# The feed-forward's shift by one token: DMA between rows of X in place of transposes there and back

## The chip, the cores and the metric

The kernel runs on one core of one Trainium2 chip. The metric is the device time of one execution in microseconds. A NeuronCore has five engines, each with an instruction stream of its own: TensorE (PE: matrix multiplications and transposes into PSUM; PEld is its weight load), VectorE (DVE), ScalarE (ACT), GpSimd (POOL) and SyncE (SP, which here issues all DMAs). Their streams meet through semaphores. DMA transfers run on 16 engines of their own. X is 4 batches of 1024 tokens with 128 channels, in float32; a tile is 128 tokens of one batch, and tokens lie on the 128 partitions of the on-chip memory (SBUF).

## The reference

After an attention block, a residual and a layernorm, six layers run on x of shape (4, 1024, 128):

```python
def shift_tokens(t):
    a, s = jnp.split(t, 2, -1)
    s = jnp.pad(s, ((0, 0), (1, 0), (0, 0)))[:, :-1]
    return jnp.concatenate([a, s], -1)

for i in range(DEPTH):   # 6
    x = attn_layer(shift_tokens(x), Wqkv[i], q_scale[i], k_scale[i], Wo[i]) + x   # 16 heads of 64, window 32
    x = ffn_layer(shift_tokens(x), ln_g[i], ln_b[i], W1[i], b1[i], W2[i], b2[i]) + x

def ffn_layer(x, g, bln, W1, b1, W2, b2):
    xn = (x - mu) / jnp.sqrt(var + 1e-05) * g + bln
    a, gate = jnp.split(xn @ W1 + b1, 2, -1)          # 2 x 341 columns
    return a * jax.nn.gelu(gate, approximate=False) @ W2 + b2
```

The shift before the feed-forward is what the change is about: channels 0 to 63 of a token stay, channels 64 to 127 come from the token before (zeros for the first token of a batch).

## The kernel before

`layers` (L872) holds the six layers. X stays in SBUF as [128 tokens, batch, tile of the sequence, channel]. Work goes in slots: slot s = 4 u + d, where u counts steps (8 blocks of 128 tokens in each of 6 layers, 48 steps) and d = 0 to 3. Each engine has its own loop over the slots (LAST_SLOT = 204) with the order of its tasks written out by hand, and the tile is processed as a pipeline over slots: in slot s tile s is projected to q, k and v, tile s-1 is rotated, normalised and transposed, tile s-2 is scored, tile s-3 attended, and tile s-4 goes through the output projection, which VectorE adds to X (`output`, L1602; semaphore `xd`). There are two PSUM tensors for pairs (PA, PB), one for the scores and the feed-forward (PC) and one for transposes and the output (PD).

The feed-forward of a step needs all four batches of it. The attention output of step u-1 is complete early in slot d = 3 of step u, and there the feed-forward starts, in these places of the loops:

- TensorE, between the lone transpose `input_T(s + 1)` (L1202) and `project_v` (L1210): `ff_shift` transposes X of four batches to PC (L1299), so that channels lie on partitions. After `project_v`: `ff_tokens` transposes back (L1308). In the slot before (d = 2) nothing stands between these.
- ScalarE: `ff_carry` (L1472) puts the last token of the step before, kept in FS, in front; `ff_shift` (L1478, L1479) copies PC to FS, channels 64 to 127 one column on.
- VectorE: `ff_tokens` (L1608) copies PC to fx; `ff_stats` (L1613 to L1621) takes mean and variance; then `input_T(s + 1)` (L1548) makes the residual of the next tile's transposed input, in two halves, for which TensorE waits at `project_qk` of the next slot; then `ff_down(u - 2)` (L1644), `ff_scale` (L1626) and, in the next slot, `sums` and `output`.
- GpSimd, at d = 0 of the next step: `frs_power` (L1108) takes the root of the variance, ahead of `norms` (L1125 to L1131), `normalise` (L1138), `divide` (L1114), `normalise`. TensorE's second group of q/k transposes (L1236) in that slot waits for the second `normalise`.
- TensorE goes on with the feed-forward one and two slots later (`ff_norm`, L1317, at d = 1).

SyncE issues DMAs in order. In a slot: `values_in(s - 1)`, four loads of VW from DRAM (L1052; each 32 rows of four pieces of 2 KB), which wait until the attention of tile s-3 has read the other buffer (semaphore `pv`); then `values_out(s)`, the store of V (L1040; 128 rows). At d = 0 a share of the next layer's weights (L1033) is loaded, and once a layer at d = 0 the feed-forward's weights and biases (L1027): W1, W2 in two pieces (the second 85 rows), b1 in three (128, 128 and 85 rows of two elements of 4 bytes), b2 (one row) and the two of the layernorm (128 rows of 4 bytes). In the first attention stage `max_rows` (L490) moves 8 rows of 256 bytes from SBUF to SBUF in each DMA.

Of the kernel before, what the change touches and what calls it, by code (L numbers as in the profile page):

```python
# [10 lines left out]
ACT = mybir.ActivationFunctionType  # L11
AX = mybir.AxisListType

P = 128
B, S, D = 4, 1024, 128
NT = S // P
# [855 lines left out]
def layers(nc, ins, w):  # L872
# [6 lines left out]
    m = Memory(nc)  # L879
    X, ident, ident_b, gate_b = w["X"], w["ident"], w["ident_b"], w["gate_b"]  # L880
# [34 lines left out]
    VW = m.sb("VW", [P, 2, NW, 512])  # L915
    ET = m.sb("ET", [P, PAIRS, P])
    OT = m.sb("OT", [P, PAIRS, P])
    FS = m.sb("FS", [P, B, P + 1])
    fx = m.sb("fx", [P, B, D])
    fst = m.sb("fst", [P, B, 6])  # L920
    fmv = m.sb("fmv", [P, B, 2])
# [49 lines left out]
    oe = m.count("l_oe")  # L971
    wo = m.count("l_wo")
    xd = m.count("l_x1")
    f1 = m.count("l_f1")
    f1e = m.count("l_f1e", 2)
    fc = m.count("l_fc")
    f2 = m.count("l_f2")
    f2e = m.count("l_f2e")
    fsd = m.count("l_fst", 3)
    fr = m.count("l_frs")  # L980
# [19 lines left out]
    def is_tile(n):  # L1000
        return 0 <= n < TILES

    def is_step(u):
        return 0 <= u < STEPS
# [8 lines left out]
    def on_sp(sp):  # L1013

        def load_ff(l):
            for dst, src in (
                (W1[:, :], ins["W1"][l]),
                (W2[:, 0:2, :], ins["W2"][l, 0:2 * P].rearrange("(a p) n -> p a n", p=P)),
                (W2[0:FF - 2 * P, 2, :], ins["W2"][l, 2 * P:FF]),
                *((b1[0:c, :, i], ins["b1"][l].rearrange("(i f) -> f i", i=2)[lo:lo + c])  # L1020
                  for i, (lo, c) in enumerate(CH)),
                (W2[LASTW:LASTW + 1, NCH - 1, :], ins["b2"][l].unsqueeze(0)),
                (ln[:, 0:1], ins["ln_g"][l].unsqueeze(1)),
                (ln[:, 1:2], ins["ln_b"][l].unsqueeze(1)),
            ):
                with nc.allow_non_contiguous_dma("small columns"):
                    sp.dma_start(dst, src).then_inc(s_wf.sem, 16)  # L1027

        def load_share(u):
            t, l = u % NT, u // NT  # L1030
            if u > 0:
                sp.wait_ge(wsp.sem, wsp.at(u - 1))
            sp.dma_start(Wraw[:, :], ins["Wqkv"][l + 1][:, t * share:(t + 1) * share]).then_inc(s_wr.sem, 16)  # L1033

        def values_out(n):
            u, b, t, l = tile(n)
            sp.wait_ge(ve.sem, ve.at(n))
            if n >= TILES // NL:
                sp.wait_ge(vw[n % 2].sem, vw[n % 2].at((n - B) // 2))
            sp.dma_start(v_dram[b, WIN + t * P:WIN + (t + 1) * P], Vs[:, :, :]).then_inc(vd.sem, 16)  # L1040

        def values_in(n):
            u, b, t, l = tile(n)
            p = n % 2
            sp.wait_ge(vd.sem, vd.at(n))
            if n >= 2:
                sp.wait_ge(pv.sem, pv.at(n - 2))
            for c in range(2):
                rows = v_dram[b, t * P + c * WIN:(t + 1) * P + c * WIN].rearrange("(v r) a n -> r v a n", r=WIN)
                for a in range(2):  # L1050
                    lo = a * KW + c * WIN
                    sp.dma_start(VW[lo:lo + WIN, p, :, :], rows[:, :, a, :]).then_inc(vw[p].sem, 16)  # L1052

        sp.wait_ge(s_one.sem, READY)
        for b in range(B):
            sp.dma_start(v_dram[b, 0:WIN], kH[0:WIN, :, :, :].rearrange("p b j k -> p (b j k)")
                         .rearrange("p (a n) -> p a n", a=2)).then_inc(s_vz.sem, 16)
        load_ff(0)
        sp.wait_ge(s_vz.sem, s_vz.at(B - 1))
        for s in range(LAST_SLOT):  # L1060
            u, d = divmod(s, B)
            if d == 0 and u < last * NT:
                load_share(u)
            if d == 0 and u % NT == 1 and u < last * NT:
                l = u // NT
                if l > 0:
                    sp.wait_ge(wo.sem, wo.at(l * NT * B - 1))
                sp.wait_ge(s_wa.sem, s_wa.at(l))
                load_attention(sp, ins, w, l + 1)
            if d == 0 and u % NT == 2 and 0 < u // NT < NL:  # L1070
                sp.wait_ge(f5.sem, f5.at(u // NT * NT - 1))
                load_ff(u // NT)
            if is_tile(s - 1):
                values_in(s - 1)
            if is_tile(s):
                values_out(s)
            if d == 2 and u == last * NT:
                sp.wait_ge(vp.sem, vp.at(B * last * NT - 1))
                sp.dma_start(XM, w["x_mid"]).then_inc(xm.sem, 16)
            if d == 2 and is_step(u - 3) and u - 3 >= last * NT:  # L1080
                sp.wait_ge(fin.sem, fin.at(u - 3 - last * NT))
                sp.dma_start(w["out_dram"][:, :, (u - 3) % NT, :], X[:, :, (u - 3) % NT, :]).then_inc(out.sem, 16)
        sp.wait_ge(out.sem, out.at(NT - 1))

    def on_pool(pool):
        pool.memset(power[:, :], -0.5).then_inc(s_one.sem, 1)
        pool.memset(kH[:, :, :, :], 0.0).then_inc(s_one.sem, 1)
        pool.memset(FS[:, :, :], 0.0).then_inc(s_one.sem, 1)
        lo = LASTW // 32 * 32
        pool.memset(zero[:, :], 0.0).then_inc(s_one.sem, 1)  # L1090
        pool.memset(three[:, :], 1.5).then_inc(s_one.sem, 1)
# [93 lines left out]
    def on_pe(pe):  # L1185
# [7 lines left out]
        def free(*banks):  # L1193
            for one in sorted(set(banks), key=lambda x: x[1]):
                pe.wait_ge(*one)
# [96 lines left out]
            mm.then_inc(wo.sem, 1)  # L1292
            fd[0] = (xd.sem, xd.at(n))

        def ff_shift(u):
            pe.wait_ge(xd.sem, xd.at(B * u + B - 1))
            free(fc_[0])
            for b in range(B):
                mm = pe.transpose(PC[:, 0, b * P:(b + 1) * P], X[:, b, u % NT, :], ident[:, :])  # L1299
            mm.then_inc(f1.sem, 1)  # L1300
            fc_[0] = (f1e.sem, f1e.at(u))

        def ff_tokens(u):
            pe.wait_ge(f1e.sem, f1e.at(u))
            pe.wait_ge(fc.sem, fc.at(u))
            free(fc_[1])
            for b in range(B):
                mm = pe.transpose(PC[:, 1, b * P:(b + 1) * P], FS[:, b, 0:P], ident[:, :])  # L1308
            mm.then_inc(f2.sem, 1)
            fc_[1] = (f2e.sem, f2e.at(u))  # L1310

        def ff_norm(u):
            pe.wait_ge(s_wf.sem, s_wf.at(u // NT))
            pe.wait_ge(fn.sem, fn.at(u))
# [33 lines left out]
        for s in range(LAST_SLOT):  # L1348
# [24 lines left out]
                attend(s - 3)  # L1373
            if is_tile(s + 1):
                input_T(s + 1)
            if d == 3 and is_step(u - 1):
                ff_shift(u - 1)
            if is_tile(s):
                project_v(s)
            if d == 3 and is_step(u - 1):  # L1380
                ff_tokens(u - 1)
            if d == 1 and is_step(u - 2):
                ff_gate(u - 2, 0)
                ff_gate(u - 2, 1)
# [5 lines left out]
    def on_act(act):  # L1390
# [73 lines left out]
            act.activation(kT[:, :, WIN:WIN + P], src, ACT.Copy).then_inc(te.sem, 1)  # L1464
            act.activation(kH[:, n % B, :, :], src[:, :, P - WIN:P], ACT.Copy).then_inc(te.sem, 1)

        def ff_carry(u):
            if u > 0:
                act.wait_ge(f2.sem, f2.at(u - 1))
                act.wait_ge(f1e.sem, f1e.at(u - 1))  # L1470
            src = FS[hc:D, :, P:P + 1] if u % NT else zero[hc:D, :].unsqueeze(2)
            act.activation(FS[hc:D, :, 0:1], src, ACT.Copy).then_inc(fc.sem, 1)  # L1472

        def ff_shift(u):
            src = PC[:, 0, :].rearrange("p (b n) -> p b n", b=B)
            act.wait_ge(fc.sem, fc.at(u))
            act.wait_ge(f1.sem, f1.at(u))
            act.activation(FS[0:hc, :, 0:P], src[0:hc], ACT.Copy).then_inc(f1e.sem, 1)  # L1478
            act.activation(FS[hc:D, :, 1:P + 1], src[hc:D], ACT.Copy).then_inc(f1e.sem, 1)  # L1479

        def ff_norm(u):
            act.wait_ge(s_wf.sem, s_wf.at(u // NT))
            act.wait_ge(f3.sem, f3.at(u))
# [21 lines left out]
        for s in range(LAST_SLOT):  # L1505
# [2 lines left out]
                ff_gate(u - 2, 1)  # L1508
            if is_tile(s):
                square(s, 0)  # L1510
            if d == 3 and is_step(u - 1):
                ff_carry(u - 1)
            if d == 2 and is_step(u - 2):
                ff_gate(u - 2, 2)
            if is_tile(s):
# [7 lines left out]
                transpose_k(s - 1)  # L1523
            if is_tile(s + 1):
                input_T(s + 1)
            if d == 3 and is_step(u - 1):
                ff_shift(u - 1)
            if d == 2 and 0 <= u < last * NT:
                split_next(u)
            if is_tile(s - 3):  # L1530
# [11 lines left out]
    def on_dve(dve):  # L1542
# [59 lines left out]
            dve.tensor_tensor(out=X[:, b, t, :], in0=PD[:, 0, 0:D], in1=X[:, b, t, :], op=ALU.add).then_inc(xd.sem, 1)  # L1602

        def ff_tokens(u):
            dve.wait_ge(f2.sem, f2.at(u))
            if u > 0:
                dve.wait_ge(f3.sem, f3.at(u - 1))
            dve.tensor_copy(fx[:, :, :], PC[:, 1, :].rearrange("p (b n) -> p b n", b=B)).then_inc(f2e.sem, 1)  # L1608

        def ff_stats(u):  # L1610
            dve.wait_ge(f2e.sem, f2e.at(u))
            for b in range(B):
                i = dve.bn_stats(fst[:, b, :], fx[:, b, :])  # L1613
            i.then_inc(fsd.sem, 1)
            dve.wait_ge(fsd.sem, fsd.at(u, 1))
            dve.memset(w["spare"][:, :], 0.0)
            for b in range(B):
                i = dve.bn_aggr(fmv[:, b, :], fst[:, b, :])
            i.then_inc(fsd.sem, 1)
            dve.wait_ge(fsd.sem, fsd.at(u, 2))  # L1620
            dve.tensor_scalar_add(fmv[:, :, 1:2], fmv[:, :, 1:2], LN_EPS).then_inc(fsd.sem, 1)  # L1621
# [24 lines left out]

        dve.wait_ge(s_one.sem, 6)
        for j in range(2):
            dve.tensor_scalar_mul(XS[:, :, j, :], FS[:, :, 0:1].broadcast_to([P, B, P + 2]), 1.0)\
                .then_inc(s_one.sem, 1)  # L1650
        dve.wait_ge(s_one.sem, READY)
        input_T(0)
# [95 lines left out]
```

## Time and profile before

| | us |
|---|---|
| median of three runs | 3981.29 |
| the runs | 3973.6 to 3982.08 |
| the profiled execution's own time | 3975.59 |
| its span, first to last instruction | 3973.6 |

| engine | busy us in the span | share |
|---|---|---|
| TensorE | 3731.3 | 94% |
| VectorE | 3272.7 | 82% |
| ScalarE | 2830.6 | 71% |
| GpSimd | 2383.9 | 60% |

The page divides the span by engine, by line and by DMA queue; a busy share is a mean over stages with different limits. The layers stage runs from about 888 us to the end. What one of its steps looks like is read from the timeline of each engine, in which instructions of one line are merged: start, duration, line, operation with its output and input, count, and in brackets the idle time before it and who ended it. All rows of one step below are from the step that begins at 2029.69 us. For DMA a window of the trace gives the number of packets by size, the share of the 16 engines' time, and for each issue the time to its landing; the 4-byte packets are either data of that size or the completions that raise the semaphore.

### The profile page before, as it was taken

Reading aid. Unit: us, or ns where it says so; the run is one execution under the profiler, and the core shown is the slowest. Engines: PE = TensorE matmul, PEld = TensorE weight load, DVE = VectorE, ACT = ScalarE, POOL = GpSimd, SP = SyncE. Lnnn points to the kernel's source line nnn. Section 1 sums busy time; section 2 is a strip of 40 time slices with the busy share of each in tenths; the row PEclk is TensorE's granted clock in tenths of the full one; section 3 lists DMA queues with packets and bytes.
Section 4 is the critical chain, followed back from the end, with each engine's and each line's share of the span. In section 5 each row is a group of like instructions: output and inputs, shape, how many; then the busy total and the mean of one; then the engine's idle time right before and its main releaser. Section 6 shows DMA issues by size and latency. Waiting matters only on the chain. (4 is left out here: it accounts for less than half of the span.)

```text
span 3973.6 us, 160814 instructions
## 1 busy us (share of the span) xinstructions
PE 3731.3 (94%) x70608; PEld 2684.1 (68%) x70608; DVE 3272.7 (82%) x4767; ACT 2830.6 (71%) x4676; POOL 2383.9 (60%) x1968
## 2 busy tenths in 40 slices
PE   5899999967999999999999999999999999999997
PEld 3222222236788878788887888878787888878775
DVE  7899999947888888888888888888888888888884
ACT  2588888856777777777777777777777777777774
POOL 2100000027777777777777777777777777777773
PEclk7799999989999999999999999999999999999998
DMA  2110000014344344344444334434444433443432
GB/s 89 32 52 23 22 18 22 10 32 114 103 106 113 102 111 117 103 105 115 108 108 114 104 100 118 114 100 107 112 109 109 114 103 103 127 109 101 114 107 55
DMA packets 202556, 360.09 MB, mean 91 GB/s; under 512 B 35518, under 2 KB 74050, under 8 KB 201538
## 3 DMA queue, kind: packets, MB, share of 16 engines
q1 hardware_dynamic: 201794, 348.71, 32.7%
q8 instruction: 627, 10.27, 1.1%
q14 instruction: 135, 1.11, 0.1%
HBM read 236.68 MB, written 111.67 MB: 88 GB/s over the span
## 5 line engine op out<-in xcount | busy, mean ns | idle before, releaser
L1120 POOL TENSOR_TENSOR T<-T 128x1024 f32<-128x1024 f32 x384 | 907.3, 2376 | 27.4 <-DVE T L1587 26.6
L1138 POOL TENSOR_TENSOR T<-T,rn 128x1024 f32<-128x1024 f32 x384 | 732.0, 1906 | 27.1 <-POOL rn L1131 0.4
L705 ACT ACTIVATE E<-p_s 128x512 f32<-128x512 f32 x1024 | 555.8, 596 | 167.9 <-PE p_s L565 162.8
L639 DVE TENSOR_REDUCE negmax<-p_max 128x1 f32<-128x1024 f32 x512 | 605.3, 1219 | 50.6 <-PE p_max L545 37.2
L1210 PE MATMUL PA<-Wqkv,XS 128*128 128x512 f32 x2304 | 632.8, 410 | 10.0 <-DVE XS L1548 7.4
L1236 PE MATMUL PD<-ident,T 128*128 128x128 f32 x3072 | 419.6, 280 | 52.5 <-ACT qT L1458 47.3
L1210 PEld LDWEIGHTS PA<-Wqkv,XS 128*128 128x128 f32 x2304 | 414.6, 193 | 79.8 <-DVE XS L1548 10.3
L1595 DVE TENSOR_REDUCE ss<-SQ 128x32 f32<-128x2048 f32 x192 | 436.9, 2275 | 0.0
L1566 DVE TENSOR_REDUCE sm<-Ew 128x16 f32<-128x1024 f32 x192 | 233.7, 1217 | 238.9 <-ACT Ew L1432 238.9
L1236 PEld LDWEIGHTS PD<-ident,T 128*128 128x128 f32 x3072 | 329.7, 141 | 115.7 <-ACT qT L1458 96.4
L1291 PEld LDWEIGHTS PD<-Wo,OT 128*128 128x128 f32 x3072 | 366.3, 192 | 61.2 <-issue 61.2
L1278 PE MATMUL PB<-ET,VW 64*64 64x32 f32 x24576 | 398.6, 220 | 6.3 <-issue 6.3
L1278 PEld LDWEIGHTS PB<-ET,VW 64*64 64x64 f32 x24576 | 376.9, 135 | 39.0 <-issue 32.3
L1418 ACT ACTIVATE SQ<-PA 128x1024 f32<-128x1024 f32 x192 | 197.1, 1027 | 271.9 <-PE PA L1210 271.9
L565 PE MATMUL p_s<-QA,KA 50*128 50x512 bf16 x1024 | 359.8, 386 | 29.5 <-ACT E L705 14.8
L1291 PE MATMUL PD<-Wo,OT 128*128 128x128 f32 x3072 | 378.7, 276 | 4.2 <-ACT OT L1444 3.1
L1114 POOL TENSOR_TENSOR Ew<-Ew,sm 128x1024 f32<-128x1024 f32 x192 | 365.9, 1906 | 12.4 <-DVE sm L1571 12.4
L545 PE MATMUL p_max<-KA,QA 48*128 48x512 bf16 x1024 | 360.7, 396 | 13.1 <-PEq L416 9.0
L1582 DVE TENSOR_TENSOR T<-PA,tab 128x1024 f32<-128x1024 f32 x192 | 234.4, 1221 | 158.9 <-ACT SQ L1418 158.9
L1210 PE MATMUL PB<-Wqkv,XS 128*128 128x512 f32 x1152 | 338.2, 429 | 0.0
L582 PE MATMUL p_o<-E,VG 128*32 128x512 f32 (+1 forms) x3832 | 321.0, 407 | 0.1
L1254 PE MATMUL PC<-kT,qT 64*32 64x64 f32 x24576 | 294.0, 224 | 23.8 <-issue 23.8
(168 smaller groups left out, 6785.0 us busy)
## 6 DMA issues: line engine op xcount, KB each, us to landing
VW<-v_rows SPq DMA_DIRECT2D x768, 256.0 KB, 4.5
v_rows<-Vs SPq DMA_DIRECT2D x192, 512.0 KB, 6.0
Wraw<-in_Wqkv SPq DMA_DIRECT2D x40, 192.0 KB, 5.1
QA<-parts_q SPq DMA_DIRECT2D x384, 16.0 KB
KA<-parts_k SPq DMA_DIRECT2D x192, 32.0 KB
parts_q<-parts SPq DMA_DIRECT2D x8, 384.0 KB, 2.6
parts_k<-parts SPq DMA_DIRECT2D x8, 384.0 KB, 2.7
Wo<-in_Wo SPq DMA_DIRECT2D x12, 256.0 KB, 4.9
```

What stands on the lines that cost most here:

```text
L545: mm = pe.matmul(p_max[:, k % 2, j * 512:(j + 1) * 512], QA[o:o + MROW, g % 3, qh, cb, qt * P:(qt + 1) * P], KA[o:o + MROW, g % 3, cb, j * ...
L565: pe.matmul(p_s[:, i % 2, :], KA[o:o + KROWS, g % 3, cb, kb * P:(kb + 1) * P], QA[o:o + KROWS, g % 3, qh, cb, :], start=True, stop=True).t ...
L639: dve.tensor_reduce(negmax[:, qh, c, qt:qt + 1], p_max[:, k % 2, :], axis=AX.X, op=ALU.max, negate=True).then_inc(s_mr.sem, 1)
L705: act.activation(E[:, s % 4, c, :], p_s[:, i % 2, :], ACT.Exp, scale=DH ** -0.5)\
L1114: pool.tensor_tensor(out=e, in0=e, in1=sm[:, p, 1, :].unsqueeze(2).broadcast_to([P, LH, KW]), op=ALU.mult).then_inc(pn.sem, 1)
L1120: pool.tensor_tensor(out=t_, in0=t_, in1=T2[:, i * HALF:(i + 1) * HALF], op=ALU.add).then_inc(ad.sem, 1)
L1138: pool.tensor_tensor(out=t_, in0=t_, in1=rn[:, p, i * LH:(i + 1) * LH].unsqueeze(2).broadcast_to([P, LH, LD]), op=ALU.mult).then_inc(no.se ...
L1210: mm = pe.matmul(pair[:, half, :], XS[:, b, i, 1:P + 1], Wqkv[:, l % 2, j, lo:lo + 512], start=(k == 0), stop=(k == 2))
L1236: mm = pe.transpose(flat(PD)[:, j * P:(j + 1) * P], T1[:, n % 2, lo:lo + P], ident[:, :])
L1278: mm = pe.matmul(PB[c * LD:(c + 1) * LD, par, i * P + q:i * P + q + WIN], VW[o:o + KW, p, v, j * LD:(j + 1) * LD], ET[o:o + KW, j, q:q + WIN],
L1291: mm = pe.matmul(PD[:, 0, 0:D], OT[:, j, :], Wo[:, l % 2, j, :], start=(j == 0), stop=(j == PAIRS - 1))
L1595: dve.reduce_sum(ss[:, p, :], heads(SQ[:, :]), axis=AX.X).then_inc(ssq.sem, 1)
```

## The change

The transposes there and back, ScalarE's copies and FS go. SyncE gets `ff_shift` at d = 3, between `values_in(s - 1)` and `values_out(s)`. It waits for `xd` (X of the step complete), for TensorE's read of fx in the step before and for its own earlier DMAs, and issues three: rows 0 to 126 of X, channels 64 to 127, to rows 1 to 127 of fx (127 rows of four pieces of 256 bytes); the row carried from the step before, from `ends`, to row 0 of fx; and row 127 of X to `ends` for the next step (`ends` has two such places and one of zeros). VectorE copies channels 0 to 63 from X to fx itself (`ff_tokens`), and `ff_stats` waits for all three DMAs (semaphore `shd`, 48 a step).

```diff
--- before.py
+++ after.py
@@ -915,7 +915,7 @@
     VW = m.sb("VW", [P, 2, NW, 512])
     ET = m.sb("ET", [P, PAIRS, P])
     OT = m.sb("OT", [P, PAIRS, P])
-    FS = m.sb("FS", [P, B, P + 1])
+    ends = m.sb("ends", [1, 3, B, hc])
     fx = m.sb("fx", [P, B, D])
     fst = m.sb("fst", [P, B, 6])
     fmv = m.sb("fmv", [P, B, 2])
@@ -971,10 +971,7 @@
     oe = m.count("l_oe")
     wo = m.count("l_wo")
     xd = m.count("l_x1")
-    f1 = m.count("l_f1")
-    f1e = m.count("l_f1e", 2)
-    fc = m.count("l_fc")
-    f2 = m.count("l_f2")
+    shd = m.count("l_shift", 48)
     f2e = m.count("l_f2e")
     fsd = m.count("l_fst", 3)
     fr = m.count("l_frs")
@@ -1050,6 +1047,17 @@
                 for a in range(2):
                     lo = a * KW + c * WIN
                     sp.dma_start(VW[lo:lo + WIN, p, :, :], rows[:, :, a, :]).then_inc(vw[p].sem, 16)
+
+        def ff_shift(u):
+
+            xt = X[:, :, u % NT, hc:D]
+            sp.wait_ge(xd.sem, xd.at(B * u + B - 1))
+            if u > 0:
+                sp.wait_ge(f3.sem, f3.at(u - 1))
+                sp.wait_ge(shd.sem, shd.at(u - 1))
+            sp.dma_start(fx[1:P, :, hc:D], xt[0:P - 1]).then_inc(shd.sem, 16)
+            sp.dma_start(fx[0:1, :, hc:D], ends[:, 1 + (u - 1) % 2 if u % NT else 0, :, :]).then_inc(shd.sem, 16)
+            sp.dma_start(ends[:, 1 + u % 2, :, :], xt[P - 1:P]).then_inc(shd.sem, 16)
 
         sp.wait_ge(s_one.sem, READY)
         for b in range(B):
@@ -1072,6 +1080,8 @@
                 load_ff(u // NT)
             if is_tile(s - 1):
                 values_in(s - 1)
+            if d == 3 and is_step(u - 1):
+                ff_shift(u - 1)
             if is_tile(s):
                 values_out(s)
             if d == 2 and u == last * NT:
@@ -1085,7 +1095,7 @@
     def on_pool(pool):
         pool.memset(power[:, :], -0.5).then_inc(s_one.sem, 1)
         pool.memset(kH[:, :, :, :], 0.0).then_inc(s_one.sem, 1)
-        pool.memset(FS[:, :, :], 0.0).then_inc(s_one.sem, 1)
+        pool.memset(ends[:, :, :, :], 0.0).then_inc(s_one.sem, 1)
         lo = LASTW // 32 * 32
         pool.memset(zero[:, :], 0.0).then_inc(s_one.sem, 1)
         pool.memset(three[:, :], 1.5).then_inc(s_one.sem, 1)
@@ -1291,23 +1301,6 @@
                 mm = pe.matmul(PD[:, 0, 0:D], OT[:, j, :], Wo[:, l % 2, j, :], start=(j == 0), stop=(j == PAIRS - 1))
             mm.then_inc(wo.sem, 1)
             fd[0] = (xd.sem, xd.at(n))
-
-        def ff_shift(u):
-            pe.wait_ge(xd.sem, xd.at(B * u + B - 1))
-            free(fc_[0])
-            for b in range(B):
-                mm = pe.transpose(PC[:, 0, b * P:(b + 1) * P], X[:, b, u % NT, :], ident[:, :])
-            mm.then_inc(f1.sem, 1)
-            fc_[0] = (f1e.sem, f1e.at(u))
-
-        def ff_tokens(u):
-            pe.wait_ge(f1e.sem, f1e.at(u))
-            pe.wait_ge(fc.sem, fc.at(u))
-            free(fc_[1])
-            for b in range(B):
-                mm = pe.transpose(PC[:, 1, b * P:(b + 1) * P], FS[:, b, 0:P], ident[:, :])
-            mm.then_inc(f2.sem, 1)
-            fc_[1] = (f2e.sem, f2e.at(u))
 
         def ff_norm(u):
             pe.wait_ge(s_wf.sem, s_wf.at(u // NT))
@@ -1373,12 +1366,8 @@
                 attend(s - 3)
             if is_tile(s + 1):
                 input_T(s + 1)
-            if d == 3 and is_step(u - 1):
-                ff_shift(u - 1)
             if is_tile(s):
                 project_v(s)
-            if d == 3 and is_step(u - 1):
-                ff_tokens(u - 1)
             if d == 1 and is_step(u - 2):
                 ff_gate(u - 2, 0)
                 ff_gate(u - 2, 1)
@@ -1464,20 +1453,6 @@
             act.activation(kT[:, :, WIN:WIN + P], src, ACT.Copy).then_inc(te.sem, 1)
             act.activation(kH[:, n % B, :, :], src[:, :, P - WIN:P], ACT.Copy).then_inc(te.sem, 1)
 
-        def ff_carry(u):
-            if u > 0:
-                act.wait_ge(f2.sem, f2.at(u - 1))
-                act.wait_ge(f1e.sem, f1e.at(u - 1))
-            src = FS[hc:D, :, P:P + 1] if u % NT else zero[hc:D, :].unsqueeze(2)
-            act.activation(FS[hc:D, :, 0:1], src, ACT.Copy).then_inc(fc.sem, 1)
-
-        def ff_shift(u):
-            src = PC[:, 0, :].rearrange("p (b n) -> p b n", b=B)
-            act.wait_ge(fc.sem, fc.at(u))
-            act.wait_ge(f1.sem, f1.at(u))
-            act.activation(FS[0:hc, :, 0:P], src[0:hc], ACT.Copy).then_inc(f1e.sem, 1)
-            act.activation(FS[hc:D, :, 1:P + 1], src[hc:D], ACT.Copy).then_inc(f1e.sem, 1)
-
         def ff_norm(u):
             act.wait_ge(s_wf.sem, s_wf.at(u // NT))
             act.wait_ge(f3.sem, f3.at(u))
@@ -1508,8 +1483,6 @@
                 ff_gate(u - 2, 1)
             if is_tile(s):
                 square(s, 0)
-            if d == 3 and is_step(u - 1):
-                ff_carry(u - 1)
             if d == 2 and is_step(u - 2):
                 ff_gate(u - 2, 2)
             if is_tile(s):
@@ -1523,8 +1496,6 @@
                 transpose_k(s - 1)
             if is_tile(s + 1):
                 input_T(s + 1)
-            if d == 3 and is_step(u - 1):
-                ff_shift(u - 1)
             if d == 2 and 0 <= u < last * NT:
                 split_next(u)
             if is_tile(s - 3):
@@ -1602,13 +1573,14 @@
             dve.tensor_tensor(out=X[:, b, t, :], in0=PD[:, 0, 0:D], in1=X[:, b, t, :], op=ALU.add).then_inc(xd.sem, 1)
 
         def ff_tokens(u):
-            dve.wait_ge(f2.sem, f2.at(u))
+            dve.wait_ge(xd.sem, xd.at(B * u + B - 1))
             if u > 0:
                 dve.wait_ge(f3.sem, f3.at(u - 1))
-            dve.tensor_copy(fx[:, :, :], PC[:, 1, :].rearrange("p (b n) -> p b n", b=B)).then_inc(f2e.sem, 1)
+            dve.tensor_copy(fx[:, :, 0:hc], X[:, :, u % NT, 0:hc]).then_inc(f2e.sem, 1)
 
         def ff_stats(u):
             dve.wait_ge(f2e.sem, f2e.at(u))
+            dve.wait_ge(shd.sem, shd.at(u))
             for b in range(B):
                 i = dve.bn_stats(fst[:, b, :], fx[:, b, :])
             i.then_inc(fsd.sem, 1)
@@ -1646,7 +1618,7 @@
 
         dve.wait_ge(s_one.sem, 6)
         for j in range(2):
-            dve.tensor_scalar_mul(XS[:, :, j, :], FS[:, :, 0:1].broadcast_to([P, B, P + 2]), 1.0)\
+            dve.tensor_scalar_mul(XS[:, :, j, :], zero[:, :].unsqueeze(2).broadcast_to([P, B, P + 2]), 1.0)\
                 .then_inc(s_one.sem, 1)
         dve.wait_ge(s_one.sem, READY)
         input_T(0)
```

## Rows read from the trace of the kernel before

**Rows 1.** Page, part 1: busy us, share of the span, instructions.

```profile
PE 3731.3 (94%) x70608; PEld 2684.1 (68%) x70608; DVE 3272.7 (82%) x4767; ACT 2830.6 (71%) x4676; POOL 2383.9 (60%) x1968
```

**Rows 2.** Timeline of TensorE: start us, us, engine, line, operation, count.

```profile
2053.24 0.33 PE L1202 MATMUL PD<-ident,X 128*128 128x128 f32 x1
2053.32 1.63 PE L1210 MATMUL PA<-Wqkv,XS 128*128 128x512 f32 x6
2054.79 1.88 PE L1333 MATMUL PC<-fnT,W 128*128 128x512 f32 x4
...
2068.87 0.33 PE L1202 MATMUL PD<-ident,X 128*128 128x128 f32 x1
...
2069.39 1.63 PE L1210 MATMUL PA<-Wqkv,XS 128*128 128x512 f32 x6
2071.16 0.66 PE L1308 MATMUL PC<-ident,FS 128*128 128x128 f32 x4
2071.65 2.84 PE L1342 MATMUL PC<-W,HH 128*128 128x128 f32 x24
2074.33 1.95 PE L1291 MATMUL PD<-Wo,OT 128*128 128x128 f32 x16
2076.04 1.63 PE L1210 MATMUL PA<-Wqkv,XS 128*128 128x512 f32 x6
...
2078.99 0.41 PE L1248 MATMUL PC<-mask,ident_b 64*32 64x512 bf16 x8
...
2082.81 1.09 PE L1236 MATMUL PD<-ident,T 128*128 128x128 f32 x8 [0.24 <-ACT qT L1458]
```

**Rows 3.** Timeline of VectorE in the same slots; in brackets the idle time before.

```profile
2060.10 0.28 DVE L1602 TENSOR_TENSOR X<-PD,X 128x128 f32<-128x128 f32 x1
...
2071.85 0.69 DVE L1608 COPY fx<-PC 128x512 f32<-128x512 f32 x1 [0.92 <-PE PC L1308]
2072.58 0.87 DVE L1613 BATCH_NORM_STATS2 fst<-fx 128x6 f32<-128x128 f32 x4
...
2073.98 0.60 DVE L1548 TENSOR_TENSOR XS<-PD,XS 64x128 fp32r<-64x128 f32 x2
```

**Rows 4.** Timeline of GpSimd in the fourth slot and after.

```profile
2074.15 1.02 POOL L1108 TENSOR_TENSOR frs<-fmv,power 128x4 f32<-128x4 f32 x1 [4.32 <-DVE fmv L1621]
...
2080.25 1.91 POOL L1138 TENSOR_TENSOR T<-T,rn 128x1024 f32<-128x1024 f32 x1
```

**Rows 5.** Timeline of SyncE (DMA issues) in the fourth slot.

```profile
2069.05 1.73 SPq L1052 DMA_DIRECT2D VW<-v_rows  x4
2073.09 0.34 SPq L1040 DMA_DIRECT2D v_rows<-Vs  x1
```

**Rows 6.** Timeline of ScalarE in the fourth slot.

```profile
2069.89 0.59 ACT L1478 ACTIVATE FS<-PC 64x512 f32<-64x512 f32 x1
```

**Rows 7.** DMA issue under way in 2070.5 to 2070.7: count, KB, us to landing.

```profile
VW<-v_rows SPq DMA_DIRECT2D x1, 256.0 KB, 5.9
```

**Rows 8.** DMA packets by size, in 308.5 to 309.2, 2053 to 2069, 2008 to 2023.

```profile
DMA packets 16, 0.00 MB, mean 3 GB/s; under 512 B 16, under 2 KB 16, under 8 KB 16
...
DMA packets 724, 1.63 MB, mean 102 GB/s; under 512 B 80, under 2 KB 80, under 8 KB 720
...
DMA packets 2274, 2.13 MB, mean 142 GB/s; under 512 B 1141, under 2 KB 1611, under 8 KB 2270
```

**Rows 9.** DMA throughput, 2016.0 to 2016.3, in 40 slices of 7.5 ns.

```profile
GB/s 71 3 3 70 3 3 70 2 2 71 3 3 71 3 2 70 4 1 70 2 2 70 2 1 2 70 1 1 70 1 2 69 69 1 69 1 1 69 1 1
```

**Rows 10.** DMA packets and share of 16 engines, 270.60 to 271.30.

```profile
DMA packets 336, 0.06 MB, mean 85 GB/s; under 512 B 330, under 2 KB 336, under 8 KB 336
...
q1 hardware_dynamic: 336, 0.06, 44.9%
```

**Rows 11.** TensorE's timeline, then a window's busy us by engine (PE first), granted clock.

```profile
902.83 2.93 PE L1210 MATMUL PA<-Wqkv,XS 128*128 128x512 f32 x6 [3.67 <-DVE XS L1548]
...
902.83:908.10 5.27, 5.27 (x12) 4.02 (x13) 1.18 (x2) 1.02 (x1) 4.76 (x6) 0.50 0.75 190
```

**Rows 12.** DMA issues of the whole span: count, KB each, median us to landing.

```profile
x_mid<-gated SPq DMA_DIRECT2D x8, 256.0 KB, 2.6
```

## Prediction

> **What bounds the kernel now.** I read the page first. TensorE is busy for 94% of the span [rows 1], and over three quarters of the span are the layers stage, where work goes in slots of one tile; four slots make a step (128 tokens of all four batches), and there are 48 steps. Then I read TensorE's timeline of one step [rows 2]. The reader is to see that each group of matmuls starts where the last one ends, so a step takes as long as its TensorE work, and that the feed-forward's shift stands in the fourth slot: it is the difference between the gaps there and the same gaps one slot earlier. Next come VectorE [rows 3] and GpSimd [rows 4] in the same slot, for how much later they may run before TensorE feels it, and last SyncE's issues [rows 5], as the new transfers have to be put between them.
>
> **What goes.** On TensorE two groups of four transposes. In the slot before, the lone input transpose is followed by the V projection after 0.08 us and that one takes 1.47 us to the next group; in the fourth slot these are 0.52 us (2068.87 to 2069.39) and 1.77 us (2069.39 to 2071.16), and the second transposes take 0.49 us more (to 2071.65) [rows 2]. So 0.44 + 0.30 + 0.49 = 1.23 us a step, the wait for ScalarE's copies included. All of it is on TensorE's path: 47 steps of it are 58 us, which is the most that the change can give. On ScalarE two copies of 0.59 us go [rows 6] and a small one; it has its tasks done early in this slot, so I count nothing. On VectorE a wait of 0.92 us and a copy of 0.69 us from PSUM become a copy of half the elements within SBUF [rows 3]; I bound that between 0 and 0.69 us, and take nothing, because it runs while VectorE waits for the transfers, below.
>
> **What comes.** Three transfers on SyncE's queue and a wait for them on VectorE, ahead of the statistics. When are they issued? X is ready early: the add that completes it starts at 2060.10 [rows 3]. But SyncE issues in order, and the code puts the shift behind the four loads of VW, which wait for the attention of this slot: SyncE issues them from 2069.05 to 2070.78 [rows 5]. So the shift goes out at 2070.78, some 10 us after its data are there. And its packets go into the same queue behind those of VW. The VW load issued last (2070.35) lands 5.9 us later, at 2076.25 [rows 7]. The shift's packets follow its packets, so I let the shift land by their own moving time later than that.
>
> How long do they move? 127 rows of 4 x 256 bytes are 508 packets. On how many of the 16 engines? That decides the case, and the packet counts of the trace answer it in part. A DMA of 8 rows shows 16 packets under 512 bytes: 8 pieces of 256 bytes and 8 completions, so 8 engines. A slot with five DMAs of 32 or 128 rows shows 80 small packets, none of which is data: 16 completions each. And the stretch in which the feed-forward's weights are loaded shows 1141 [rows 8]. Of these 938 are data of four bytes (b1 goes as two columns: 2 x (128 + 128 + 85) = 682, and ln as 2 x 128 = 256). That leaves 203 completions. It has 12 DMAs of 32 or 128 rows (4 VW, V, Wraw, two of W, two of b1, two of ln) for 192, one of a single row, and two of 85 rows; 192 + 1 + 5 + 5 = 203. So 85 rows went on 5 engines, 8 on 8, 32 and 128 on 16: the largest number up to 16 by which the rows divide. 127 is prime. By that pattern all 508 packets go through one engine; no row of this trace has such a count itself.
>
> The Trainium skill ("DMA: Bandwidth & Descriptors", section "Why a DMA increments its semaphore by 16 and not by 1") gives this as the rule, the largest count up to 16 that divides the slowest dimension on both sides, and names 127 partitions as a case of one engine; the three counts agree with it, and that it holds for 127 no run shows yet.
>
> One engine's pace: at the end of a load of 85 rows only one engine is still at work with pieces of 512 bytes, and there is a peak of 70 GB/s in every third slice of 7.5 ns, one piece each 23.5 ns [rows 9]. For pieces of 256 bytes and less, 336 packets took 44.9% of 16 engines over 0.70 us, which is 5.03 us, or 15.0 ns each [rows 10]. I take 15.0 ns, since most of these have this size or half of it. Ends: half of 23.5 (11.75 ns, if only bytes counted) and 23.5 itself. So the shift moves for 508 x 15.0 ns = 7.6 us (6.0 to 11.9) and lands at 2083.85 (2082.2 to 2088.2). The two small transfers of four pieces each go with it. If SyncE can't get rid of them before the long one has drained, they land a free-queue DMA's time later, 2.6 us [rows 12]; I take 0 and keep 2.6 for the range. What is queued behind the shift on SyncE is the store of V (2073.09 before [rows 5]) and the share of the next weights; the store is next needed one slot later, with over 10 us to go, and I count nothing.
>
> By the skill's same page (section "Why small descriptors are slow (HBM only)") a piece of 256 bytes costs 11 cycles where one of 512 costs 19, and moves within SBUF don't bear the overhead; that would be an estimated 6.0 to 6.9 us in place of 7.6, some 30 to 75 us less in all, which stays within the range.
>
> **What the landing does.** Before, the statistics start at 2072.58 [rows 3]. Behind the wait on VectorE stand: the statistics, the residual of the next input's transpose (done 2.00 us after the statistics begin: 2072.58 to 2074.58), the feed-forward's last add, the scaling and the sums. Who waits: TensorE for that input (its projections at 2076.04) and GpSimd for the variance. New: the input is ready at 2083.85 + 2.05 = 2085.9. TensorE reaches its projections at about 2074.8 (2076.04 less 1.23) and stands idle for 11.1 us. What comes then is late in two ways. GpSimd: the root starts 1.57 us after the statistics and the third normalisation ends 8.01 us after it (2074.15 to 2082.16) [rows 4], so at L + 9.6, with L the landing. TensorE: projections in 2.95 us (2076.04 to 2078.99) and 3.82 us on to the second q/k transposes at 2082.81 [rows 2], so at L + 8.8 at full clock. But after an idle stretch the clock is down: once TensorE had been idle for 3.67 us, the 12 matmuls of the two projections ran at a granted clock of 0.50 (1.2 GHz) and filled 5.27 us (from 902.83) [rows 11], 2.32 us more. An idle stretch three times as long will do no less. So TensorE gets there at L + 11.14, behind which GpSimd's L + 9.6 is hidden. Against 2082.81 that is 2083.85 + 11.14 - 2082.81 = 12.2 us later, the saved 1.23 us already in it. From there the slot's work is TensorE's again, at its old pace.
>
> **Sum.** 46 steps have a next tile's input behind the shift: 46 x 12.2 = 561 us. The last two run in the drain, where the chain is latency: I estimate 9 us and 5 us (no VW ahead in the last). Sum 575 us. The profiled execution took 3975.6 us (span 3973.6 and 2.0 us around it), so 4550.6; the median shown lies 5.7 us above that execution: 4556.
>
> **Rivals.**
> 1. The transfer is spread over 16 engines. For it: every large DMA of this trace is; against it: the 85 rows. 32 packets each, 0.5 us, landing 2076.75. TensorE idles for 4.0 us. If the clock falls, 5.1 us a step and 235 us in all, else GpSimd's 9.6 decides, 3.5 us a step and 161. With 5 us for the drain: 4147 to 4221. Chance 0.10.
> 2. The other side: the transfers are hidden and the transposes' time is won. The point from which it decides is the landing: with GpSimd's L + 9.6 against 2082.81 it is even at L = 2073.2, which is 2.4 us after the issue at 2070.78; the full 58 us (3923) want it within 1.2 us. It would need the shift's packets to pass VW's. For it: a DMA of 256 KB lands in 2.6 us with nothing ahead [rows 12]; against it: one queue, and VW occupies it for 5 us. Chance 0.04, half of that for within 0.2%.
> 3. One engine and worse: 23.5 ns a packet adds 4.3 us a step, 199 us: 4755; with the small transfers 2.6 us later 120 more: 4875. Above 4800 I give it 0.06.
> 4. One engine but cheaper: with 11.75 ns 1.65 us a step less (4480), and with the clock staying up, so that L + 9.6 decides, 1.54 us less again: 4409. It is part of the forecast.
>
> **How the numbers follow.** The likeliest is one engine, in any of its sizes between 4409 and 4800, with 0.80 (the middle 4556). Below that stand rivals 1 and 2 with 0.14, above it 0.06; together 0.20 are left out, so the range is 4409 to 4800. Some 0.2% (8 us) is what a measurement of this kernel can tell from no change. Faster 0.02, within it 0.02, slower 0.96.
>
> **What would show it.** In the profile after: the VectorE statistics (now L1613's line) are preceded in each step by an idle stretch of some 12 us that a DMA ends; the landing of the 127-row transfer is some 12 to 13 us from its issue; its pieces follow one another at about 15 ns with 1 of 16 engines busy; the granted clock is below full in every step, with projections of 2.7 us; TensorE's busy share falls to near 85%. If that landing is 5 to 6 us, rival 1 is right; if the projections keep 1.5 us, the clock term is wrong; if the shift's packets mix with VW's, the queue term is. The prediction is wrong at its root if VectorE's wait is under 2 us.

## The result, and the profile after

The changed kernel takes 4489.17 us (median of four runs, 4479.58 to 4496.34) where the kernel before takes 3981.68 us beside it: a ratio of 1.1268, with a 95% interval of 1.1228 to 1.1308. That is 507 us slower. The forecast was 4556 us with a range of 4409 to 4800.

The profiled execution has a span of 4494.6 us. First the page: busy us, share of the span and instructions of each engine, and the costliest groups with the idle time before them.

```profile
PE 3801.2 (85%) x70224; PEld 2724.3 (61%) x70224; DVE 3251.5 (72%) x4767; ACT 2762.5 (61%) x4532; POOL 2382.8 (53%) x1968
...
L1220 PE MATMUL PA<-Wqkv,XS 128*128 128x512 f32 x2304 | 695.2, 441 | 456.5 <-DVE XS L1519 452.7
...
L1585 DVE BATCH_NORM_STATS2 fst<-fx 128x6 f32<-128x128 f32 x192 | 41.9, 280 | 551.7 <-DMA ends<-X 551.7
```

TensorE's share fell from 94% [rows 1] to 85%. The span grew by 521 us (3973.6 to 4494.6), and most of that is one wait of TensorE: 452.7 us before the projections, for the next tile's input from VectorE, which itself stood idle for 551.7 us in 48 waits (11.5 us each) for the transfers.

One step: VectorE, SyncE's issues, TensorE and GpSimd in the fourth slot and after it. The columns are as in rows 2 to 5, which the lines answer.

```profile
2340.41 0.29 DVE L1579 COPY fx<-X 128x256 f32<-128x256 f32 x1
2352.45 0.87 DVE L1585 BATCH_NORM_STATS2 fst<-fx 128x6 f32<-128x128 f32 x4 [11.75 <-DMA ends<-X]
```

```profile
2338.61 1.73 SPq L1049 DMA_DIRECT2D VW<-v_rows  x4
2340.45 0.72 SPq L1058 DMA_DIRECT2D fx<-X  x1
2341.22 8.89 SPq L1059 DMA_DIRECT2D fx<-ends  x1
2350.15 0.57 SPq L1060 DMA_DIRECT2D ends<-X  x1
```

```profile
2342.68 1.95 PE L1301 MATMUL PD<-Wo,OT 128*128 128x128 f32 x16
2354.51 2.93 PE L1220 MATMUL PA<-Wqkv,XS 128*128 128x512 f32 x6 [9.88 <-DVE XS L1519]
2357.23 2.71 PE L1220 MATMUL PB<-Wqkv,XS 128*128 128x512 f32 x6
...
2363.70 1.09 PE L1246 MATMUL PD<-ident,T 128*128 128x128 f32 x8 [0.24 <-ACT qT L1447]
```

```profile
2354.02 1.02 POOL L1118 TENSOR_TENSOR frs<-fmv,power 128x4 f32<-128x4 f32 x1 [14.61 <-DVE fmv L1593]
...
2360.11 1.90 POOL L1148 TENSOR_TENSOR T<-T,rn 128x1024 f32<-128x1024 f32 x1
```

The loads of VW begin at 2338.61 here and at 2069.05 before [rows 5]; counted from there, the second q/k transposes come 25.09 us later and came 13.76 us later before [rows 2]: 11.3 us for this step. The reader is to see the chain: the transfer goes out right behind VW, it is 12.0 us from its issue (2340.45) to the statistics (2352.45), TensorE's projections follow 2.06 us after these, and they take 2.7 us each. In the next step the wait is as long, but the second of the two projections is fast again:

```profile
2428.35 2.93 PE L1220 MATMUL PA<-Wqkv,XS 128*128 128x512 f32 x6 [9.60 <-DVE XS L1519]
2431.08 1.76 PE L1220 MATMUL PB<-Wqkv,XS 128*128 128x512 f32 x6
```

Last, what the DMA engines do while everything waits: throughput in 40 slices of 0.15 us, packets, and share of the 16 engines, from 2345 to 2351 us.

```profile
GB/s 17 19 17 19 19 17 19 19 17 19 17 19 19 17 19 19 17 19 17 19 19 17 19 19 17 19 17 19 19 17 19 19 17 19 17 19 19 17 24 19
DMA packets 431, 0.11 MB, mean 18 GB/s; under 512 B 431, under 2 KB 431, under 8 KB 431
...
q1 hardware_dynamic: 431, 0.11, 8.0%
```

A flat 18 GB/s: one piece of 256 bytes each 13.9 ns (6.0 us by 431, a few of them completions), for as long as the stretch lasts. The share of 8.0% of 16 engines is 1.3 engines, or 17.8 ns of busy time for each packet. One engine whose packets overlap a little fits this; the trace doesn't name the engine.

The throughput from 2343.6 to 2345.6 us, in slices of 0.05 us, shows where the transfer begins:

```profile
GB/s 410 123 410 205 164 451 82 287 287 82 41 574 0 0 11 10 10 10 10 20 5 10 15 20 10 20 15 20 15 20 15 20 15 20 15 20 15 20 20 15
```

The last 2 KB pieces of VW move up to 2344.2, and the first piece of 256 bytes follows at 2344.32, which is 3.87 us after the issue of the shift. The load of VW issued last lands only at 2345.27. The last pieces of 256 bytes, those of the small transfers included, move at 2351.69, 0.76 us before the statistics.

### The profile page after: what moved, and what is told of

The parts are those of the page before. It is cut to its first block, busy times and chain, and to the rows that moved or that the text cites. A ratio compares the mean times of both kernels' runs of the same rounds, so it can differ in the third digit from the quotient of the medians.

```text
span 4494.6 us, 159949 instructions
## 1 busy us (share of the span) xinstructions
PE 3801.2 (85%) x70224; PEld 2724.3 (61%) x70224; DVE 3251.5 (72%) x4767; ACT 2762.5 (61%) x4532; POOL 2382.8 (53%) x1968
## 3 DMA queue, kind: packets, MB, share of 16 engines
q14 instruction: 136, 1.11, 0.1%
## 4 chain that ended last, share of the span: by engine, by line
PE 55%; SPq 12%; ACT 5%; DMA 2%; DVE 2%; issue 2%; POOL 1%; POOLq 0%; DVEq 0%; ACTq 0%
PE PA L1220 12%; SPq L1059 9%; PE PD L1246 9%; PE PB L1288 9%; PE PB L1220 7%; PE PD L1301 6%; PE PC L1264 6%; ACT qT L1447 4%; PE PC L1326 3%; PE PC L1319 3%; DMA ends<-X 2%; SPq L1049 2%; PE PC L1258 1%; DVE fst L1585 1%; PE PD L1212 1%
## 5 line engine op out<-in xcount | busy, mean ns | idle before, releaser
L1220 PE MATMUL PA<-Wqkv,XS 128*128 128x512 f32 x2304 | 695.2, 441 | 456.5 <-DVE XS L1519 452.7
L1220 PEld LDWEIGHTS PA<-Wqkv,XS 128*128 128x128 f32 x2304 | 454.6, 212 | 545.3 <-DVE XS L1519 466.0
L1585 DVE BATCH_NORM_STATS2 fst<-fx 128x6 f32<-128x128 f32 x192 | 41.9, 280 | 551.7 <-DMA ends<-X 551.7
L1118 POOL TENSOR_TENSOR frs<-fmv,power 128x4 f32<-128x4 f32 x48 | 48.8, 1017 | 710.6 <-DVE fmv L1593 710.6
L1220 PE MATMUL PB<-Wqkv,XS 128*128 128x512 f32 x1152 | 373.0, 464 | 0.0
```

The source lines that it names most:

```text
L1220: mm = pe.matmul(pair[:, half, :], XS[:, b, i, 1:P + 1], Wqkv[:, l % 2, j, lo:lo + 512], start=(k == 0), stop=(k == 2))
```

## The experiments

The kernel before took 3982.20 us beside e1 to e4 and 3979.71 us beside e5 to e8; across these groups the ratios compare better than the times.

| kernel | us | ratio to before, 95% interval |
|---|---|---|
| the change | 4489.17 | 1.1268 (1.1228 to 1.1308) |
| e1: 112 + 15 rows, late | 4230.36 | 1.0616 (1.0600 to 1.0631) |
| e2: 127 rows, early | 3924.96 | 0.9853 (0.9837 to 0.9870) |
| e3: 112 + 15 rows, early | 3934.04 | 0.9872 (0.9857 to 0.9886) |
| e4: small transfers first, late | 4486.52 | 1.1262 (1.1245 to 1.1279) |
| e5: no transfer | 3924.10 | 0.9853 (0.9833 to 0.9873) |
| e6: TensorE filled while it waits | 4438.74 | 1.1147 (1.1118 to 1.1176) |
| e7: 122 + 5 rows, late | 4329.19 | 1.0882 (1.0849 to 1.0915) |
| e8: 122 + 5 rows, early | 3933.25 | 0.9880 (0.9857 to 0.9904) |

**e1, over how many engines.**

```diff
-            sp.dma_start(fx[1:P, :, hc:D], xt[0:P - 1]).then_inc(shd.sem, 16)
+            sp.dma_start(fx[1:P - 15, :, hc:D], xt[0:P - 16]).then_inc(shd.sem, 16)
+            sp.dma_start(fx[P - 15:P, :, hc:D], xt[P - 16:P - 1]).then_inc(shd.sem, 16)
```

> The 127 rows go as two DMAs, of 112 and of 15 rows, in the same place behind the loads of VW. Theory A (the wait is long because one DMA engine moves all 508 pieces): 112 rows go on 16 engines (28 pieces each), 15 on 15 (4 each), moving time 0.5 us in place of 7.2; landing some 6 us after the issue in place of 12.0; what stays is the place behind VW. About 3 to 4.5 us a step over the kernel before in place of 11.3: 4120 us if the clock stays up, 4190 if it falls. Rival B (the wait is the queue behind VW, whatever the count of engines): no change, 4489 us. Rival C (the last small transfer, held back on SyncE, sets it): one DMA more to issue, so 4489 us or slightly more.

It took 4230 us: 259 us less than the change with the same bytes in the same place, one DMA more. VectorE's wait in one step, and SyncE's issues before it:

```profile
2240.64 0.87 DVE L1586 BATCH_NORM_STATS2 fst<-fx 128x6 f32<-128x128 f32 x4 [6.72 <-DMA ends<-X]
```

```profile
2233.68 0.68 SPq L1058 DMA_DIRECT2D fx<-X  x1
2234.40 0.94 SPq L1059 DMA_DIRECT2D fx<-X  x1
2235.39 0.67 SPq L1060 DMA_DIRECT2D fx<-ends  x1
2236.10 0.60 SPq L1061 DMA_DIRECT2D ends<-X  x1
```

So rival B is out: how the rows are cut into DMAs sets half of the loss (259 of 507 us). Rival C this run can't exclude, since SyncE's hold went with the long transfer (0.94 us at the second issue, 8.89 in the change); e4 below does. It missed theory A's upper end of 4190 us by 40 us: the landing came 6.96 us after the issue (2233.68 to 2240.64) and not some 6. The packets say a part of it. Of the 516 pieces of 256 bytes, 484 have moved by 2238.5; the other 32 move from then to 2239.8, while all engines together move 364 GB/s (2238.5 to 2240.0), for the store of V and the next weights, issued behind the shift at 2236.81 and 2237.24. That these hold them up is likely, and no run tested it.

**e7, a third count of engines.** The same edit with 122 and 5 rows.

> The 127 rows in two DMAs, of 122 and of 5 rows, in the change's late place. By the pattern (the largest number up to 16 that divides the rows) 122 rows = 2 x 61 go on 2 engines, 244 pieces each at 14.2 ns, 3.5 us in place of 7.2: landing 3.7 us earlier than with one engine, 3.7 us a step, 4489 - 172 = 4317 us. If only prime counts went to one engine and others were spread widely, it would be as fast as 112 + 15 rows, 4230 us. If the number of pieces alone counted, not the engines, 4489 us.

It took 4329 us, between the two, and 12 us from the forecast. The throughput line of its window 2275.0 to 2277.0 (slices of 0.05 us) ends in a flat 36 GB/s, twice that of the change, and VectorE's wait in this step is 3.7 us shorter than the 11.75 us there:

```profile
GB/s 246 123 451 164 205 287 410 87 231 62 108 108 31 21 26 26 20 31 31 20 10 26 26 31 36 36 36 36 41 31 41 36 36 36 36 36 36 36 36 36
```

```profile
2280.03 0.87 DVE L1586 BATCH_NORM_STATS2 fst<-fx 128x6 f32<-128x128 f32 x4 [8.09 <-DMA ends<-X]
```

So the count of rows sets the pace as [rows 8] had suggested: 127 rows move at 18 GB/s, 122 at 36. Over all 48 steps VectorE waits for the transfers 11.5 us each in the change (551.7 in all), 8.1 in e7 (390.1) and 6.3 in e1 (300.2).

**e2, the place in SyncE's order.**

```diff
+            if d == 3 and is_step(u - 1):
+                ff_shift(u - 1)
             if is_tile(s - 1):
                 values_in(s - 1)
-            if d == 3 and is_step(u - 1):
-                ff_shift(u - 1)
```

> The shift as in the change, 127 rows in one DMA, but issued ahead of the loads of VW on SyncE, when X is complete (some 8.7 us earlier in the slot). Theory A: the 508 pieces still take 7.2 us on one engine, with no VW ahead of them; they land some 9.5 us after the issue, about 1.5 us before VectorE asks for them; no wait is left and the transposes' time is won: 3923 us. SyncE is held by the second transfer for some 8 us, so VW is issued about 1 us later than before, which has over 5 us of slack. Rival B (queue behind VW): 3923 us too, with a landing about 3 us after the issue. Rival C (SyncE's hold costs): VW late, TensorE waits for it in each fourth slot, 4000 us or more.

It took 3924.96 us: 1.5% faster than the kernel before, 564 us faster than the change, by two lines in another place. SyncE and VectorE in one step:

```profile
2042.50 0.74 SPq L1058 DMA_DIRECT2D fx<-X  x1
2043.29 6.49 SPq L1059 DMA_DIRECT2D fx<-ends  x1
2049.83 0.57 SPq L1060 DMA_DIRECT2D ends<-X  x1
2051.14 1.74 SPq L1049 DMA_DIRECT2D VW<-v_rows  x4
```

```profile
2052.93 0.28 DVE L1579 COPY fx<-X 128x256 f32<-128x256 f32 x1
2053.25 0.87 DVE L1585 BATCH_NORM_STATS2 fst<-fx 128x6 f32<-128x128 f32 x4
```

The transfer is as slow as before: mostly 18 GB/s in slices of 0.1 us from 2045 to 2048 us. But it goes out at 2042.50, when X is complete, 8.6 us before the loads of VW, and no idle time stands before the statistics any more (only in the last step of all, which has nothing to hide it behind, VectorE waits 8.13 us). SyncE is held here as well, for 6.49 us, but it has nothing to do in that stretch: VW goes out at 2051.14, right behind this slot's last attention matmuls and 0.18 us after the input transpose that follows them on TensorE (2050.96 in its timeline), as before (2069.05 against 2068.87 [rows 2, 5]).

**e5, no transfer at all.**

```diff
-            dve.tensor_copy(fx[:, :, 0:hc], X[:, :, u % NT, 0:hc]).then_inc(f2e.sem, 1)
+            dve.tensor_copy(fx[:, :, :], X[:, :, u % NT, :]).then_inc(f2e.sem, 1)
```

> The change without its three transfers and without the wait for them: VectorE copies all 128 channels of X to fx, unshifted (this kernel leaves the feed-forward's shift out of the computation). It measures what the transposes, the copies and their waits are worth on TensorE's path: 1.23 us in each of 47 steps, 58 us under the kernel before, 3923 us. If the early transfer costs nothing at all, this is not faster than the run that has it (3925 us) by more than 3 us. A rival reading of 3925 us, that the early transfers still cost something hidden, would give 3915 us or less here.

It took 3924.10 us, a ratio of 0.9853 just as e2's. So the transposes' worth on TensorE is some 57 us (58 by the prediction's sum; in the traces a step goes from 62.94 to 61.83 us, which is 1.11 us and not 1.23). The early transfer costs nothing that these runs can tell (61.82 us a step in e2): e2 has all that there was to win.

**e3 and e8, early and spread.**

> Both: two DMAs of 112 and 15 rows, issued ahead of the loads of VW. All theories: landing about 3 us after the issue, no wait left, 3923 us. If this is faster than the shift in one early DMA by more than 5 us, the hold of SyncE or a late landing costs something there.

> The same two DMAs of 122 and 5 rows, in the early place. 127 rows in one DMA gave 3925 us there, 112 + 15 rows 3934, with the scores of the fourth slot taking 1.62 us in place of 1.46 while the pieces move. If that comes from the burst of small pieces on all engines, two engines give 3925 us; if it comes from a fourth DMA and its issue, 3934 us.

Both times came out some 9 us above e2's, at 3934 and 3933 us, against e3's expectation of 3923. The intervals of the ratios overlap with e2's in part, so the times alone don't show a difference. The traces do for e3: its steps take 62.05 us, e2's 61.82 (mean distance from one step's statistics to the next one's). One group on TensorE differs: the scores of the fourth slot take 1.62 us in place of 1.46 while the pieces move, 0.16 us in 48 steps, or 8 us. From 1000 to 3880 us, e3's line and e2's:

```profile
L1265 PE MATMUL PC<-kT,qT 64*32 64x64 f32 x23808 | 292.3, 224 | 27.0 <-issue 26.7
```

```profile
L1264 PE MATMUL PC<-kT,qT 64*32 64x64 f32 x23808 | 284.2, 224 | 25.5 <-issue 25.5
```

In e8 that group takes 286.5 us by the same view, and its steps take 61.83 us, as in e2. What its profiled execution lost (3931.03 us against 3925.77), it lost ahead of the layers, where the two kernels are the same. The last scores of the first attention stage, in e8 and in e2 (shortest, median and longest ns, then the start of the first and the last in us):

```profile
L565 PE MATMUL p_s<-QA,KA x1024: 376/386/631, 136.4 to 846.4; 50*128 50x512 bf16 x171
```

```profile
L565 PE MATMUL p_s<-QA,KA x1024: 376/386/631, 137.5 to 840.3; 50*128 50x512 bf16 x171
```

That is 6.1 us. So e8's time, which by its expectation speaks for a cost of the fourth DMA, shows no such cost in the steps; what moves the first stage stays open (in the change's profiled execution it ends late too, with the last scores at 847.1 where before has 838.3). How small pieces on many engines would slow TensorE, as in e3, stays open as well.

**e4, is it the small transfer?** In the change the profile names `ends<-X` as what ended VectorE's wait.

```diff
+            sp.dma_start(fx[0:1, :, hc:D], ends[:, 1 + (u - 1) % 2 if u % NT else 0, :, :]).then_inc(shd.sem, 16)
+            sp.dma_start(ends[:, 1 + u % 2, :, :], xt[P - 1:P]).then_inc(shd.sem, 16)
             sp.dma_start(fx[1:P, :, hc:D], xt[0:P - 1]).then_inc(shd.sem, 16)
```

> As the change, but the two small transfers (rows of ends) are issued ahead of the one of 127 rows. The profile names the last small one as what ends VectorE's wait. Theory A (the long transfer's own moving time sets the landing; the small ones only come after it): the long one is issued 1 us later but starts behind VW as before, so 4489 us within 15 us. Rival C (the small one is late because SyncE is held for 8.7 us ahead of it, and lands 2.3 us after its issue): the wait gets shorter by up to 2.3 us a step, 4380 us.

It took 4486.52 us, no change. The profile now names `fx<-X`, and SyncE is held at the next DMA, here the store of V:

```profile
2332.97 0.70 SPq L1060 DMA_DIRECT2D fx<-X  x1
2333.78 7.31 SPq L1037 DMA_DIRECT2D v_rows<-Vs  x1
```

```profile
2343.20 0.87 DVE L1585 BATCH_NORM_STATS2 fst<-fx 128x6 f32<-128x128 f32 x4 [11.28 <-DMA fx<-X]
```

So rival C is out too: the hold on SyncE is a sign of the long transfer and, here, no cost of its own.

**e6, the clock's part.**

```diff
             if is_tile(s):
+                if d == 0 and u >= 2:
+                    free(*fa)
+                    for k in range(44):
+                        pe.matmul(PA[:, k % 2, 0:P], ident[:, :], ident[:, :], start=True, stop=True)
                 project_qk(s, 0)
```

> The change, late transfer on one engine as it is, with 44 matmuls of 128x128 of the identity added on TensorE where it waits for the next input (d = 0, before the projections), some 9.4 us of work in an idle stretch of 9.9 us; their result is overwritten. Theory (a part of the loss is the clock that falls while TensorE idles): the projections run at 2.4 GHz, 2.95 us in place of 5.3, and now GpSimd's third normalisation decides, L + 9.6 in place of L + 11.2: 1.6 us a step less, 74 us in all, 4415 us. Rival (all of the loss is the wait for the transfer, the clock costs nothing): 4489 us or a little more.

It took 4438.74 us. TensorE and GpSimd after the wait:

```profile
2314.01 9.99 PE L1353 MATMUL PA<-ident 128*128 128x128 f32 x88
2323.75 1.65 PE L1220 MATMUL PA<-Wqkv,XS 128*128 128x512 f32 x6
2325.24 1.55 PE L1220 MATMUL PB<-Wqkv,XS 128*128 128x512 f32 x6
...
2331.39 1.06 PE L1246 MATMUL PD<-ident,T 128*128 128x128 f32 x8 [0.80 <-POOL T L1148]
```

```profile
2323.26 1.02 POOL L1118 TENSOR_TENSOR frs<-fmv,power 128x4 f32<-128x4 f32 x1 [14.33 <-DVE fmv L1597]
```

The trace has two records for each of the 44 matmuls. The mechanism is as expected: more work on TensorE makes the kernel 50 us faster (4439 against 4489; 48 by the ratios). The projections run at full clock (1.49 and 1.48 us from start to start in place of 2.72 and 2.65), and now the second transposes wait for GpSimd, 8.13 us after its root began. What the expectation calls GpSimd's third normalisation is its second `normalise`, the one behind `divide`. The size is smaller than the 74 us forecast, since the clock had cost less than I thought (next section).

## Why the prediction was right

**The cause** held: one engine for 508 pieces, read from the packet counts of three stretches [rows 8]. The change shows 18 GB/s, e7 36, and e1 takes 259 us away. That is the step on which rival 1 (4147 to 4221 us) hung, and e1 is that rival made real, at 4230 us. The size came out too large: a loss of 575 us was forecast and 507 measured. Two terms were too large, the landing and the clock, so the two didn't cancel each other.

**The place in the queue** held: e2 and e5 show that the same slow transfer costs nothing that they can tell when it is issued as soon as X is there. Rival 2 put the break-even at a landing 2.4 us after the late issue; moving the issue 8.6 us forward was the other way to get there, and I had not listed it as one.

**The landing** was over-sized by 1.07 us: 13.07 us from issue to landing by the sum (2070.78 to 2083.85), 12.00 measured. The sum let the first piece wait for VW's landing, 5.47 us after the issue. It moved after 3.87, since VW's landing comes after its last packet has moved and the next packets don't wait for it: 1.60 us less. All 516 pieces moved in 7.37 us and not 7.6: 0.2 less. The pace was 13.9 ns where the sum had 15.0; that figure was the engines' busy time per packet [rows 10], which in the change is 17.8 ns, so busy time doesn't give the pace. And the 0.76 us from the last pieces to the statistics were missing from the sum. These three make the 1.07, so the landing is closer than its parts were. 46 steps of it are 49 us.

**The path behind the landing** held for the step shown: second transposes at L + 11.14 forecast, L + 11.25 measured (2352.45 to 2363.70), with L the start of the statistics. But the clock's term varies from step to step, and I took it from one place, with the words that a longer idle stretch "will do no less". It did less. The two projections take between 4.3 and 5.4 us, in 18 of 46 steps under 4.8, and then the second one is fast, as in the rows from 2428.35 on (1.69 us from start to start, where 1.48 is full clock). What decides when it comes back, no run shows. The projections' busy time over the whole kernel went from 971.0 us (632.8 + 338.2 on the page of before) to 1068.2 us (695.2 + 373.0), 97 us or 2.0 us a step where I had 2.32: 15 us. It also explains e6: over 46 steps the second transposes start at L + 10.9 in the mean in the change and at L + 9.7 in e6, which is 1.2 us a step or 55 us, and 50 were measured.

With these two, 4556 - 49 - 15 = 4492 us, against 4489. The first of them is from one step, but all 46 steps of the trace say the same: from the first issue of VW to the second transposes the sum has 25.94 us, the mean is 24.56, and 46 times 1.38 are 64 us. The drain, forecast at 14 us, is 14.2 by the traces (from the second transposes of the 46th step to the end, 126.6 us before and 140.8 after). The saved transposes are no term of this sum, because TensorE waits in any case; e5 measured them. That ScalarE, VectorE's copy and the later store of V cost nothing was not tested by itself.

On the rules: by the Trainium skill ("DMA: Bandwidth & Descriptors", section "Why a DMA increments its semaphore by 16 and not by 1"), 127 partitions are a case of one engine; the change's flat 18 GB/s and e7's 36 for 122 rows agree with it. Its other section cited, "Why small descriptors are slow (HBM only)", keeps moves within SBUF free of the overhead of small pieces; here the measurement speaks against it: 13.9 ns for 256 bytes within SBUF is 18 GB/s, where pieces of 512 bytes moved at 23.5 ns, or 22 GB/s [rows 9]. The ratio of 0.59 is near the 11 to 19 cycles that the prediction worked out with that section's formula (0.58) and not the 0.5 of the bytes. The pieces of 512 bytes came from DRAM, though, and no run moved such pieces within SBUF.

## What to carry to other kernels

Look at the row count of every DMA before its bytes: here 127 rows moved at 18 GB/s, 122 at 36, and splitting off 15 rows took the mean wait from 11.5 to 6.3 us. Then ask where the issue stands in its queue: the data were ready 10 us before the issue, and moving two lines turned 13% slower into 1.5% faster. And where TensorE is the bound, a wait on it can cost more than its length: here the projections behind it ran at a mean granted clock of 0.56, and took 2.0 us more a step.

## What was not expected of the hardware

SyncE was held at the issue that follows the one-engine transfer: 8.89 us in the change, 6.49 us in e2, 7.31 us in e4, and with 122 rows, at the issue of the 5 rows, 5.01 us in the late place (2272.50 to 2277.51 in e7's timeline) and 2.79 in the early one (e8); after 112 rows 0.94 us. In the change it is freed at 2350.11, 1.6 us before the last pieces move (2351.69). And filling TensorE's wait with 9.99 us of matmuls made the kernel 50 us faster, with the mean granted clock of the run back from 0.922 to 0.98.
